# Graph attention on one core: the first four heads' exponentials in the mask's slot, and their transpose through DRAM and VectorE

## The reference

```python
h = jnp.maximum(_layernorm(x, axis=-1), 0.0)
q = split_heads(h @ Wq + bq); k = split_heads(h @ Wk + bk); v = split_heads(h @ Wv + bv)
scores = einsum('bhqd,bhkd->bhqk', q, k) / sqrt(32) + beta * adj
scores = where(adj > 0, scores, -9e15)
out = x + einsum('bhqk,bhkd->bhqd', softmax(scores), v)
```

## Time and profile before

| what | value |
|---|---|
| median of 3 runs | 535.08 us (534.84 to 535.11) |
| profiled execution, its own time | 535.0 us |
| its span | 533.1 us |
| TensorE busy | 520.9 us, 98% |
| TensorE weight load busy | 438.7 us, 82% |
| VectorE busy | 451.9 us, 85% |
| ScalarE busy | 462.3 us, 87% |
| granted clock of TensorE | 1.00 of full speed |

### The profile page before, as it was taken

One profiled execution on the slowest core, in us unless ns is written; L12 is line 12 of the kernel. 1 busy time (PEld: TensorE's weight loads), 2 busy tenths in 40 slices (PEclk: granted clock), 3 DMA queues, 4 the chain that ended last, 5 costly groups with the idle time before them and its releaser, 6 DMA issues.

```text
span 533.1 us, 17434 instructions
## 1 busy us (share of the span) xinstructions
PE 520.9 (98%) x5394; PEld 438.7 (82%) x5394; DVE 451.9 (85%) x2285; ACT 462.3 (87%) x1856; POOL 127.3 (24%) x204
## 2 busy tenths in 40 slices
PE   8989999999999999999999999999999999999995
PEld 8768888888888888888888888888888888888774
DVE  6788998888898898898888889888889987765896
ACT  3558899999999999999999999998998999888984
POOL 4522222212212222221221222222122111101211
PEclk9999999999999999999999999999999999999999
DMA  7523374654646465464645556364565434222111
GB/s 238 186 81 91 115 215 123 201 154 133 192 137 188 123 170 176 123 192 140 189 134 149 177 143 192 128 188 133 138 189 161 128 116 123 71 80 75 51 56 46
DMA packets 89671, 75.25 MB, mean 141 GB/s; under 512 B 39056, under 2 KB 86288, under 8 KB 89616
## 3 DMA queue, kind: packets, MB, share of 16 engines
q1 hardware_dynamic: 89616, 74.62, 46.5%
HBM read 40.37 MB, written 34.21 MB: 140 GB/s over the span
## 4 chain that ended last, share of the span: by engine, by line
PE 90%; DVE 2%; issue 1%; DVEq 0%
PE G_ps L797 35%; PE S_ps L868 18%; PE PT_ps L852 17%; PE S_ps L817 10%; PE PT_ps L834 9%; DVE probsT L682 1%; DVE probs L651 0%; PE G_ps L852 0%; PE PT_ps L858 0%; DVE outT L634 0%; PE S_ps L878 0%; DVE y L701 0%; PE S_ps L894 0%; DVE y L669 0%; DVE qk L621 0%
## 5 line engine op out<-in xcount | busy, mean ns | idle before, releaser
L481 ACT ACTIVATE probs<-probs,negmax 128x128 f32<-128x128 f32 x768 | 298.1, 397 | 0.1
L651 DVE CUSTOM_DVE_ANT_0 probs<-S_ps,bias 128x128 f32<-128x128 f32 x768 | 164.2, 283 | 3.3 <-PE S_ps L817 3.3
L481 ACT ACTIVATION_READ_ACCUMULATOR probs<-probs,negmax 128x1 f32 x768 | 150.2, 196 | 0.0
L452 POOL TENSOR_TENSOR y<-y,x_ring 128x384 f32<-128x384 f32 x63 | 63.4, 1007 | 343.6 <-DVE y L669 343.6
L797 PE MATMUL G_ps<-h_hi,w_lo 128*128 128x512 f32 x288 | 117.7, 409 | 0.0
L797 PE MATMUL G_ps<-h_hi,w_hi 128*128 128x512 f32 x288 | 117.7, 409 | 0.0
L797 PE MATMUL G_ps<-h_lo,w_hi 128*128 128x512 f32 x288 | 116.2, 403 | 0.0
L489 ACT COPY probsT<-PT_ps 128x512 f32<-128x512 f32 x181 | 99.9, 584 | 12.0 <-PE PT_ps L852 11.4
L852 PE MATMUL PT_ps<-ident,probs 128*128 128x128 f32 x728 | 103.6, 277 | 0.0
L852 PEld LDWEIGHTS PT_ps<-ident,probs 128*128 128x128 f32 x728 | 81.9, 141 | 10.3 <-issue 1.0
L868 PE MATMUL S_ps<-w_hi,h_hi 128*128 128x384 f32 x192 | 65.2, 339 | 0.0
(11 more groups left out here) (57 smaller groups left out, 603.6 us busy)
## 6 DMA issues: line engine op xcount, KB each, us to landing
out_dram<-y SPq DMA_DIRECT2D x63, 192.0 KB, 1.9
x_ring<-in_x_dram SPq DMA_DIRECT2D x15, 768.0 KB, 5.4
out_rows<-out_blocks SPq DMA_DIRECT2D x58, 192.0 KB, 1.9
out_moved<-out_rows SPq DMA_DIRECT2D x232, 48.0 KB, 2.1
xhat_rows<-xhat_blocks SPq DMA_DIRECT2D x26, 384.0 KB, 2.6
xhat_moved<-xhat_rows SPq DMA_DIRECT2D x104, 96.0 KB, 2.7
adj_in<-in_adj_dram SPq DMA_DIRECT2D x16, 256.0 KB, 3.2
x_ring<-in_x_dram SPq DMA_DIRECT2D x4, 192.0 KB, 3.2
```

The source lines that it names most:

```text
L452: nc.gpsimd.tensor_tensor(y[:, z.s % 2 ^ d, :], y[:, z.s % 2 ^ d, :], x_ring[:, bass.ds(at, D)], ALU.add).then_inc(y_ready, 1)
L481: last = nc.scalar.activation(p, p, ACT.Exp, bias=negmax[:, e, j * KC + m:j * KC + m + 1], scale=TURN, accum_out=rowsum[:, e, m * HC + j:m ...
L651: last = nc.vector.tensor_tensor_reduce(probs[:, a, j, m, :], S_ps[:, j, m * N:(m + 1) * N], bias[(z.par + 1) % 2][:, z.s, :], 1.0, LARGES ...
```

## The change

Slots of the flag `Q` (all with scores and projections, but the last) now have the exponentials of block 0 right after their own mask (`exponentials_ahead`), written in blocks to `probs_blocks`. SP writes these to `probs_rows` in DRAM, reads them back in the next slot in four parts with the 32-row blocks exchanged, and VectorE transposes the 32x32 blocks into probsT (`transpose_probs`). There TensorE's transposes of block 0 and ScalarE's copy of them go (`R`). Slots of `F` keep them. On VectorE, the reciprocals come first in the slot, and the mask ahead of hT and `normalise`. Unit 2 of qk is stored by ScalarE. On SP, x comes in four loads per group, adj one slot later. At the start, x's first four sequences are loaded ahead of the weights, the idle matmuls are fewer, low parts are made one by one, group 0's last transpose of xhat goes ahead of its last projections, and group 0's unit 5 is stored by ScalarE. At the end, the copies of probsT and outT are shared between VectorE and ScalarE, and the reciprocals are taken in one.

```diff
 MASK_ORDER = [1, 0, 2, 3]
 RING = 8
+LOADS = [[0], [1, 2], [3], []]
 QK_UNITS = 6
...
 STORE_1 = [[], [1], [], [4]]
 STORE_2 = [[0], [], [3], []]
-STORE_V = [[], [2], [], [5]]
-WARM = [8, 4, 4, 6, 8]
+STORE_0 = [[], [], [2], []]
+STORE_V = [[], [], [], [5]]
+WARM = [8, 2, 2, 3, 7]
 SPLIT_ORDER = [0, 1, 2, 3, 4, 6, 5, 7, 8]
...
 mask_term = sb("mask_term", [P, N])
 bias = [sb(f"bias{i}", [P, GROUP, N]) for i in range(2)]
 probs = sb("probs", [P, 2, HC, KC, N])
+FOUR = HC * HD
+probs_blocks = sb("probs_blocks", [P, HC * FOUR])
+probs_rows = nc.dram_tensor("probs_rows", [2, P, HC * FOUR], F32, kind="Internal").ap()
+probs_moved = sb("probs_moved", [P, 2, HC * FOUR])
 v = sb("v", [P, 2, D])
 negmax = sb("negmax", [P, 2, HEADS])
 rowsum = sb("rowsum", [P, 2, HEADS])
...
         sp.dma_start(w_raw[:, :, c * D + first:c * D + last], w.rearrange("(k p) n -> p k n", p=P)[:, :, first:last]).then_inc(landed, 16)
-    for q in range(2):
+    for q in range(GROUP):
         load_first(q)
     load_weights(0, wq, 0, P, w_first)
-    for q in range(2, GROUP):
-        load_first(q)
     load_weights(0, wq, P, D, w_loaded[0])
+    load_first(GROUP)
     with nc.allow_non_contiguous_dma(reason="bias columns, once"):
...
     sp.dma_start(beta_col[:, :], beta.rearrange("(a n) -> a n", a=1).broadcast_to([P, 1])).then_inc(const_loaded, 16)
-    sp.dma_start(x_ring[:, GROUP * D:2 * GROUP * D].rearrange("p (s d) -> p s d", s=GROUP), x_v[:, 1, :, :]).then_inc(x_loaded[1], 16)
     load_weights(1, wk, 0, D, w_loaded[1])
+    sp.dma_start(x_ring[:, (GROUP + 1) * D:2 * GROUP * D].rearrange("p (s d) -> p s d", s=GROUP - 1), x_v[:, 1, 1:, :]).then_inc(x_loaded[1], 16)
     load_weights(2, wv, 0, D, w_loaded[2])
...
             sp.dma_start(goes, came).then_inc(blocks_moved[pair], 16)
     def slot(z):
+        if z.R:
+            sp.wait_ge(probs_rows_written, 16 * (z.e + 1))
+            for c in range(HC):
+                came = probs_rows[(z.s - 1) % 2, :, c * FOUR:(c + 1) * FOUR].rearrange("(r p) n -> p r n", r=HC)
+                goes = probs_moved[c * HD:(c + 1) * HD, (z.s - 1) % 2, :].rearrange("p (r n) -> p r n", r=HC)
+                sp.dma_start(goes, came).then_inc(probs_blocks_moved[(z.s - 1) % 2], 16)
         if z.W:
             sp.wait_ge(outT_stored, z.o + 1)
             sp.dma_start(out_rows[z.s % 2, :, :], out_blocks[:, :]).then_inc(out_rows_written, 16)
-        if z.T and z.s == 0:
-            if started(z.groups(0)):
-                sp.wait_ge(bias_ready, z.count(0))
-            sp.dma_start(adj_in[(z.par + 1) % 2][:, :, :],
-                         adj_v[:, bass.ds(z.groups(1), 1), :, :].rearrange("q g s k -> q (g s) k")).then_inc(adj_loaded[(z.par + 1) % 2], 16)
-        if z.s == 1 and not (z.static and z.groups(3) >= NG):
-            sp.wait_ge(stats_ready, z.count(1))
-            sp.dma_start(x_ring[:, bass.ds(z.ring(3, 0), GROUP * D)].rearrange("p (s d) -> p s d", s=GROUP),
-                         x_v[:, bass.ds(z.groups(3), 1), :, :].rearrange("t g s d -> t (g s) d")).then_inc(x_loaded[(z.par + 1) % 2], 16)
         if not (z.static and not 1 <= z.groups(0) <= NG - 3):
             if z.s % 2 == 1:
                 sp.wait_ge(xhat_ready, order(z.count(2)) + 1)
...
         if z.M and z.s == 0:
             sp.wait_ge(rows_written[1], 16 * z.groups(-1))
             read_blocks(1)
+        if z.T and z.s == 1:
+            if started(z.groups(0)):
+                sp.wait_ge(bias_ready, z.count(0) - 1)
+            sp.dma_start(adj_in[(z.par + 1) % 2][:, :, :],
+                         adj_v[:, bass.ds(z.groups(1), 1), :, :].rearrange("q g s k -> q (g s) k")).then_inc(adj_loaded[(z.par + 1) % 2], 16)
+        if not (z.static and z.groups(3) >= NG):
+            if z.s == 0:
+                sp.wait_ge(stats_ready, z.count(1) + 2)
+            for q in LOADS[z.s]:
+                sp.dma_start(x_ring[:, bass.ds(z.ring(3, q), D)],
+                             x_v[:, bass.ds(z.groups(3), 1), q, :].rearrange("t g d -> t (g d)")).then_inc(x_loaded[(z.par + 1) % 2], 16)
+        if z.Q:
+            sp.wait_ge(probs_ready[0], z.a + 1)
+            sp.dma_start(probs_rows[z.s % 2, :, :], probs_blocks[:, :]).then_inc(probs_rows_written, 16)
         if z.W:
             sp.wait_ge(out_rows_written, 16 * (z.o + 1))
...
                                         accum_out=rowsum[:, e, m * HC + j:m * HC + j + 1])
         last.then_inc(probs_ready[m], 1)
+    def exponentials_ahead(z):
+        act.wait_ge(masked, z.a + 1)
+        if started(z.a - 1):
+            act.wait_ge(rinv_ready, z.a - 1)
+        if started(z.a):
+            act.wait_ge(probs_rows_written, 16 * z.a)
+        a = z.s % 2
+        blocks = probs_blocks.rearrange("p (c j e) -> p j c e", c=HC, j=HC)
+        for j in range(HC):
+            last = nc.scalar.activation(blocks[:, j, :, :], probs[:, a, j, 0, :].rearrange("p (c e) -> p c e", c=HC), ACT.Exp,
+                                        bias=negmax[:, a, j * KC:j * KC + 1], scale=TURN, accum_out=rowsum[:, a, j:j + 1])
+        last.then_inc(probs_ready[0], 1)
     def store_probsT(z, m):
-        act.wait_ge(pT_in_psum[m], z.e + 1)
-        if m == 0 and started(z.e):
+        act.wait_ge(pT_in_psum[m], transposed(z, m))
+        if (z.F or m == 1) and started(z.e):
             act.wait_ge(pv_done, z.e)
         nc.scalar.copy(probsT[:, m, :], pT_bank(z, m)).then_inc(pT_stored[m], 1)
...
                              hT_of(z).rearrange("p (k t) -> p k t", k=KC), ACT.Relu).then_inc(h_hi_stored, 1)
     def slot(z):
+        if z.L:
+            act.wait_ge(third_pv, KC)
+            nc.scalar.copy(outT[:, (KC - 1) * N:], outT_last(KC - 1)).then_inc(third_outT[KC - 1], 1)
         if z.T and not z.P:
             high_part(z)
         if z.E:
-            exponentials(z, 0)
+            if z.F:
+                exponentials(z, 0)
             exponentials(z, 1)
-            if not (z.F and not z.A):
+            if z.F and z.A:
                 store_probsT(z, 0)
+        if z.P:
+            for u in STORE_0[z.s]:
+                store_qk(z, u)
+        if z.E:
             exponentials(z, 2)
+            if z.F and not z.A:
+                store_probsT(z, 2)
         if z.P:
             for u in STORE_1[z.s]:
                 store_qk(z, u)
+        if z.Q:
+            exponentials_ahead(z)
         if z.M:
...
             store_probsT(z, 1)
-        if z.X and z.A:
+        if z.X and z.P and z.between:
             high_part(z)
...
         if z.P:
-            for u in STORE_2[z.s]:
+            for u in STORE_2[z.s] + STORE_V[z.s] * (z.static and z.groups(0) == 0):
                 store_qk(z, u)
-        if z.X and z.P and not z.A:
+        if z.X and z.P and not z.between:
             high_part(z)
         if z.static and z.T and not z.P and z.s == 1:
...
     def store_probsT(z, m):
-        dve.wait_ge(pT_in_psum[m], z.e + 1)
+        dve.wait_ge(pT_in_psum[m], transposed(z, m))
         dve.wait_ge(pv_done, z.e)
         nc.vector.tensor_copy(probsT[:, m, :], pT_bank(z, m)).then_inc(pT_stored[m], 1)
+    def transpose_probs(z):
+        dve.wait_ge(probs_blocks_moved[(z.s - 1) % 2], 64 * (z.moved_before() + 1))
+        if started(z.e):
+            dve.wait_ge(pv_done, z.e)
+        nc.vector.transpose(probsT[:, 0, :].rearrange("p (j r e) -> p r j e", j=HC, r=HC),
+                            probs_moved[:, (z.s - 1) % 2, :].rearrange("p (r j e) -> p r j e", r=HC, j=HC)).then_inc(pT_stored[0], 1)
     def last_output(z):
-        dve.wait_ge(normalised, z.o)
-        for m in range(KC):
-            hs = slice(m * HC, (m + 1) * HC)
+        reciprocals(z)
+        dve.wait_ge(out_in_psum, z.o - FIRST_F)
+        for m in range(KC - 1):
             dve.wait_ge(third_pv, m + 1)
-            dve.wait_ge(out_in_psum, z.o - FIRST_F)
-            nc.vector.tensor_copy(outT[:, m * N:(m + 1) * N], outT_last(m)).then_inc(third_outT, 1)
-            if m == 0:
-                dve.wait_ge(probs_ready[2], z.o + 1)
-            nc.vector.reciprocal(rinv[:, z.s % 2, hs], rowsum[:, z.s % 2, hs]).then_inc(third_rinv, 1)
+            nc.vector.tensor_copy(outT[:, m * N:(m + 1) * N], outT_last(m)).then_inc(third_outT[m], 1)
         dve.wait_ge(out_written[z.s % 2], 16 * z.written(0))
+        dve.wait_ge(rinv_ready, z.o + 1)
         x_last = x_ring[:, z.place(z.o)[1]:z.place(z.o)[1] + D]
         for m in range(KC):
             cols, hs = slice(m * P, (m + 1) * P), slice(m * HC, (m + 1) * HC)
-            dve.wait_ge(third_rinv, m + 1)
             dve.wait_ge(third_out, m + 1)
             nc.vector.tensor_tensor(y[:, z.s % 2, cols].rearrange("p (h d) -> p h d", d=HD), outT_last(m).rearrange("p (h d) -> p h d", d=HD),
...
                     statistics(q, q)
                     if q > 0:
                         normalise(z, q - 1)
+                low_part(z)
                 normalise(z, GROUP - 1)
                 weights_low(0)
         if z.L:
...
             return
```

(77 more changed lines are left out.)

63 lines of the change are left out of this document (38 added, 25 removed).

## The result

The changed kernel takes 561.0 us in the median of four runs (559.33 to 564.66), the kernel before, on the same chip, 535.1 (534.84 to 535.25): ratio 1.0494, 95% interval 1.0438 to 1.055. The prediction, 529.2 us and faster, is wrong by 31.8 us and in its sign, and the result lies far outside its range. The profiled execution took 559.9, its span is 557.7.

The account below looks back on a forecast made before the run. TensorE, 98% busy, bounds the kernel; afterwards ScalarE's loop of 7.85 us replaces its 7.84. Loop +0.5 and ends -6.4 give -5.9 on a 533.1 us span, 527.2; forecast 529.2 us, 8 in 10 within 519 to 541.

Parts of the forecast that it names:

- the way through DRAM: Exponentials written out by SP and read back for VectorE's transpose in the next slot: the two trips cost nothing.
- 1.1 us in hand: Reads land 4.3 us into the next slot at the latest, VectorE wants them at 5.4: 1.1 us to spare.
- Landing: The 256 KB write of exponentials lands in 2.1 us, taken from 1.9 for 192 KB and 2.6 for 384 KB.
- The start of the reads: SP starts reading the exponentials back about 8.1 us after the scores' start; the last read lands by 12.1.
- rival C: DRAM trip late, VectorE waits, scores follow; decides from 1.1 us longer; 2 us longer costs 0.45 per slot, 555 us; chance 0.16.
- rows 7: Profile rows cited: between 60 and 80 us the kernel before moved 211 GB/s, share 0.72, TensorE never idle.
- ScalarE's 7.85: Loop from scores through mask, early exponentials, h_hi, copies and products with v to next scores: 7.85 us, bounds 7.66 to 7.96.
- VectorE's 7.78: VectorE's loop from scores through mask, new transpose and low part to the next scores: 7.78 us a slot.
- TensorE's 7.42: TensorE's own period per slot without block 0's transposes: 7.84 less 0.42, so 7.42 us.
- rival A: TensorE's loss counts in full, the 52 slots of groups 2 to 14 fall to 7.42 us: 507 us; chance 0.10.
- Rival B: Loops at their long end, 7.96 to 8.0 us, with waits for several semaphores: 536 us, no change; chance 0.12.
- The ends: Start, groups 0, 1 and 15, and tail, outside the 52 slots of groups 2 to 14: -6.4 us in sum.

Follow-up runs that it names:

- e1: Changed kernel without the trip through DRAM: VectorE transposes straight from ScalarE's blocks in two buffers, 32-row exchange left out, so another output; 532.01 us.
- e3: Changed kernel with adj's and x's loads behind the four out_moved reads, and xhat's rows' write behind the exponentials' write; 570.41 us.
- e6: Changed kernel with adj's and x's loads moved on SP ahead of its wait for xhat; 547.33 us.
- e15: e8 with the exponentials' write to DRAM issued by ScalarE in place of SP; 535.76 us.
- e7: e6 with, in group 1 alone, the exponentials' write ahead of SP's wait for the second xhat; 545.15 us.
- e8: e7 with each early exponential waiting for its own bank of the mask, in the mask's order; 539.36 us.
- e9: e8 with the store of y issued at the end of ScalarE's slot in place of SP's; 543.4 us.
- e13: e8 with the loads of adj and x issued at the end of ScalarE's slot in place of SP's; 538.84 us.
- e16: e8 with both the exponentials' write and the store of y on ScalarE's queue; 540.34 us.
- e4: Changed kernel with x in one 768 KB load per group in slot 1, ahead of the exponentials' write; 592.5 us.
- e17: e15 with, in group 1, SP's wait for xhat and its rows' write behind the four out_moved reads; 534.17 us.
- e18: Changed kernel with only the exponentials' write issued by ScalarE in place of SP; 571.05 us.

## Why the prediction was wrong

**The failed step is the way through DRAM**, costed at nothing with "1.1 us in hand". e1, without it, takes 532.0, 2.8 over the forecast; with it the kernel takes 561.0. Three of its terms were mis-sized, all for slot 1:
- The exponentials end 5.5 after the scores, and the step let SP issue at that moment. It issued at 7.0. Ahead of the write stand a wait for xhat, which the change puts behind the mask on VectorE (SP idle 1.7 us), and four issues. The prediction counted SP's issues as an average (6.5 of 7.8 us; this slot's, from 307.86 to 317.04, are 6.5 us too, and 7.4 with what lies between them but for the idle 1.7) and asked what is queued behind the new waits, but not what is queued ahead of the new write.
- Landing: 2.1 us was interpolated between the medians for 192 KB and 384 KB. Behind 1 MB of other transfers it took 3.98, and 2.9 as a median. A median hides what stands ahead of a transfer. The trace of the kernel before had both cases for the write of xhat's rows, alone and right behind x's load:
```profile
211.24 0.32 SPq L355 DMA_DIRECT2D xhat_rows<-xhat_blocks  x1
xhat_rows<-xhat_blocks SPq DMA_DIRECT2D x1, 384.0 KB, 2.3
...
226.61 0.41 SPq L380 DMA_DIRECT2D x_ring<-in_x_dram  x1
227.14 0.43 SPq L355 DMA_DIRECT2D xhat_rows<-xhat_blocks  x1
xhat_rows<-xhat_blocks SPq DMA_DIRECT2D x1, 384.0 KB, 5.8
```
- The start of the reads: 8.1 by the forecast, with the last landing at 12.1. Here they only start at 11.0, and they do so in e3 too, where the write leaves and lands as forecast.

The reads are 2.9 us late, past the 1.1 from which rival C decides. C was the mechanism, and had a chance of 0.16. Its price per slot for a trip 2 us late, 0.45, is near what the loop lost (22.1 us in 52 slots, 0.43 each), which is partly luck, since the trips are not equally late. Its 555 is low all the same: it has nothing for group 1, where one slot took 12.67 and the whole 5.8 us more than before. The evidence was in hand: rows 7 gave the load, the two landings above its effect, and a term that rests on 1.1 us needed slot 1 written out instruction by instruction.

The Trainium skill (DMA: Bandwidth & Descriptors, section Latency and other measured facts) gives HBM's access latency as 0.2 us on average and 2 us at high load; by that a late trip would come from its landing. The runs put most of it elsewhere: e6 and e15 carry the same 106.20 MB at a higher rate (195 and 199 GB/s over the span, 190 in the changed kernel) and regain 13.7 us and, with e7's and e8's edits, 25.2. The landing did grow with what stood ahead of it (2.0 in e3's slot 1, 3.9 in the changed kernel's), in the direction that the page gives. But it is as long in e6, which regains the 13.7.

**The loops were right.** ScalarE's 7.85: undisturbed slots of 7.81 in e1, 7.89 in e6 and e7. VectorE's 7.78: 7.75 once ScalarE's loop is shortened. TensorE's 7.42 shows in group 14 of e8, where VectorE has no statistics to make (7.39 to 7.57), and in group 15 (7.39 to 7.57). The 128x512 transpose was put at 0.61; its starts are 0.63 apart from the next (303.51 to 304.14 in e7). ScalarE waits 0.63 and 1.21 for the mask in two slots of e7 (forecast 0.5 to 1), TensorE 0.16 to 0.41 for the copy (0.3 to 0.5). So next to nothing comes from taking the transposes off TensorE, as forecast, and rival A (507) is refuted by e1: TensorE was at 98%, and with 24.8 us off its work the loop did not get shorter. The Trainium skill, Perfetto Trace Analysis, section Identifying the Most-Contended Engine, would have the engine with the highest occupancy relieved first, but TensorE judged by its weight loads and not by its matmuls. The trace agrees with that reserve: TensorE's weight loads were at 82%, below ScalarE's 87%. Rival B (a loop of 7.96 to 8.0) did not come.

**The ends.** In e1, against before: first scores -1.83 (forecast -2.1), group 1 -0.71 (-1.6), group 15 -1.53 (-1.7), end -0.6 (-1.0): -4.7 in place of -6.4. The loop gave +1.5 (+0.5), most of it from the first slots of groups 2 to 11, 7.94 to 8.42, where most others are 7.80 to 7.84. With the span these make e1's -3.1.

**What stays open**: ScalarE's idle 2.9 to 3.4 us at the jump in e9, e13 and e16; the 0.08 us by which slots of e7 are longer than e1's in groups 2 to 11 (there the distance from the last mask to the first early exponential is 0.41 against 0.33; in the unrolled groups it is 0.33 in both, and slots of 7.80 are found in both); how much of the loss in e3 and e4 is TensorE's clock; and which of e17's early slots is late for what. Its gain over before, 0.45%, is measured; that it is 1.6 us better than e15 is within the spread of the two.

## What to carry to other kernels

A transfer with about 1 us in hand has to be followed through its queue instruction by instruction in the fullest slot: what is issued ahead of it, and which wait stands ahead with whose due time. An average share of the queue and a median landing time do not bound it. If a step is moved to an engine, first see whether that engine's own loop has anything in hand; two limits must be taken away together, and each cure alone may show as a loss. And 25 us off an engine at 98% shorten the loop by nothing if the relief closes a loop of the same length through two others.

## What the hardware showed that was not expected

- Order alone on one DMA queue moved the kernel by 13.7 us (561.0 to 547.3) at the same bytes and issues, and by 9.4 us in the other direction (e3), part of that through TensorE's clock.
- A 256 KB write landed in 2.1 us as a median with the loads and the rows of xhat behind it (e3), 2.9 in the changed kernel, and 3.98 behind 1 MB issued in the 2.3 us before it. A 384 KB write landed in 2.3 us alone and in 5.8 right behind a 768 KB load, in the kernel before.
- One of SP's issues takes 0.4 to 0.5 us from start to start, but single ones stretched: one read took 1.29 in e15 at 61.24.
- ScalarE stood idle for 0.46 us where it had to wait for its own last exponential before it issued the write (e15, e18). In the three runs in which it issued transfers whose address depends on the loop's counter (e9, e13, e16), 2.9 to 3.4 us passed behind the jump of the hardware loop, and 0.2 in e8 and e15.
- After waits TensorE was granted less clock for some us: 0.51 from 55.7 to 60.0 in the changed kernel, 0.61 from 293.6 to 298 in e3.
